# A gated attention and expert kernel on Trainium2: key and query weights multiplied on the chip, and the first stage's five queues in another order

## The chip, the cores and the metric

The kernel runs on one core of one Trainium2 chip. The metric is the device time of one execution in microseconds (us), from the launch's first to its last instruction on that core, the median over several executions. Engines are named as in the profile: PE is TensorE (matrix products and transposes), PEld its weight loads, DVE is VectorE, ACT is ScalarE, POOL is GpSimd, SP is SyncE, which here only starts DMA transfers. Each engine works through its own queue in order; engines wait for each other by semaphores.

## The reference, cut to what matters

Four blocks follow each other on `x` (8 batches of 256 tokens of 256 numbers), each added to `x` with a gain. The change touches the first; what it computes:

```python
# _layernorm(x) is q_in; ctx_512 (8, 120, 128) is key and value input
q = jnp.einsum('bld,de->ble', q_in, Wq) + bq
k = jnp.einsum('bld,de->ble', ctx_512, Wk) + bk
v = jnp.einsum('bld,de->ble', ctx_512, Wv) + bv
scores = jnp.einsum('bqe,bke->bqk', q, k)
attn = jax.nn.softmax(scores, axis=-1)
x = x + jnp.tanh(g_xattn[0]) * jnp.einsum('bqk,bke->bqe', attn, v)
```

The second block is a mixture of experts: logits of 12 experts per token, the best two chosen, eight of the experts real two-layer networks of width 512. The third is attention with 16 heads, the fourth one linear layer in 8-bit floats.

## The kernel before, in words

The first stage of the program does the first attention for the eight batches and, beside it, what the experts need: the logits, and the expert weights (8 MB, loaded in eight 1 MB pieces into `wl`) split into a rounded part `wh` and a rest `wl`. The split has 32 chunks of 512 columns: ACT writes `wh` of chunk j (`high(j)`, L667), and then the rest is written over `wl`: by POOL (`low(j)`, L512, 28 chunks), or by DVE (`low(j)`, L1045, the four chunks of `VECTOR_LOW`). A rest waits for its own high (`split_h`). No expert may start before all 32 are split.

A batch b passes through these steps. DVE takes the mean and variance of its two tiles (`stats0`, L984 to L992), POOL the inverse root (`root0`, L496, L498), ACT applies them (`norm0`, L648). PE transposes the result (`transpose_x0`, L1576), ACT copies it (`copy_xT`, L629). Keys: PE multiplies the context by the key weights (`keys0`, L1550), ACT adds the bias (`copy_kt0`, L622), PE multiplies by the query weights and by the query bias (`keys_by_query`, L1561, L1564), DVE copies both (`copy_kq`, L1004, `copy_bqk`, L1008). PE makes the scores (`scores0`, L1590 with the bias row, L1596), DVE the maximum (`max0_of`, L1019), ACT the exponential (`exp0_of`, L635), PE its transpose (`transpose_prob`, L1605), ACT the copy (`copy_probT`, L642), PE the product with the values (`attend`, L1613; values by `values0`, L1571, and `copy_v0`, L1013). DVE divides and adds to `x` (`add_x1`, L1025, L1028). Then the second norm: `stats1` on DVE (the same lines as `stats0`), `root1` on POOL (the same lines as `root0`), `norm1` on ACT (L657). PE transposes (`transpose_x1`, L1576), DVE copies (`copy_xT1`, L1039), PE multiplies by the gate (`gate_of`, L1630), DVE adds the bias (`logits_of`, L1049). In between ACT once starts five DMAs that clear the expert output (`clear_y`, L680, L683).

The order on each engine is written by hand: every engine has a loop over steps t, and in step t it serves batch t minus an offset of its own. ACT serves `norm1(t - 6)`, POOL `root1(t - 5)`. Highs and lows are strewn between by tables (`HIGH_FROM`, `LOW_FROM`, `LOW_LATE`): ACT does up to four highs a step, from step 2, POOL up to three or four lows.

At the stage's end twelve products for the third block (`products1`, L1638 and L1641 on PE, L722 and L726 on ACT) are fitted in; PE does the first three in the loop and five more ahead of the counting product (L1689, L1692). DVE then picks the two best experts of each token (L1069 to L1133), PE counts (L1689, L1692), DVE turns the counts into slots, beginning with `rows_up` (L1145), and ends with `slot_i` (L1173) and `blk_i` (L1180). POOL gathers by `slot_i` as soon as its lows are done. The experts start behind that.

Of the kernel before, what the change touches and what calls it, by code (L numbers as in the profile page):

```python
# [23 lines left out]
P = 128  # L24
# [66 lines left out]
def build(nc, x, ctxT, wq0T, wk0, wv0, bq0, bk0, bv0, gateT, gbias, wmoe, wq1, wk1, wv1, wo1,  # L91
          bq1, bk1, bv1, bo1, wfT, bf, gains, c_ident, c_tri, c_count, c_token, c_head, out):
    ctx = ExitStack()
    with ctx:
# [87 lines left out]
        kt0 = sb("kt0", [P, 2, C, LK], F32, att)  # L182
# [111 lines left out]
        def sems(names):  # L294
# [11 lines left out]
        (kt_done, kt_ok, kq_done, kq_ok, bqk_ok, v0_done, v0_ok) = sems(  # L306
            "kt_done kt_ok kq_done kq_ok bqk_ok v0_done v0_ok")
# [7 lines left out]
        split_h, split_l, split_d = sems("split_h split_l split_d")  # L315
# [80 lines left out]
        IN_CTX, IN_CON, IN_CST = 16 * 3, 16 * 4, 16 * 6  # L396
# [9 lines left out]


        HIGH_FROM, LOW_FROM = (8, 2, 2, 2), (4, 4, 9, 3)
        EARLY, FAR = TILES - 2 * U, 64 * P
        AHEAD, ZERO_LOADS = 6, 1 + 2 * TILES * D // ZEROS  # L410
        VECTOR_LOW, VECTOR_FROM = (7, 10, 13, 16), 5
        LOW_LATE = {B: 3, B + 1: 4, B + 2: 3, B + 3: 2, B + 4: CHUNKS}
# [61 lines left out]
        def _(pool):  # L474
            pool.dma_start(ident[:], c_ident).then_inc(cst_in, 16)
# [38 lines left out]
            pieces = iter(j for j in range(CHUNKS) if j not in VECTOR_LOW)  # L514

            def low_next(t, k):

                if t >= LOW_FROM[k]:
                    for j in itertools.islice(pieces, 1):
                        low(j)  # L520

            for t in range(B):
                low_next(t, 0)
                low_next(t, 1)
                root0(t)
                low_next(t, 2)
                low_next(t, 3)
                if 0 <= t - 5:
                    root1(t - 5)
            for t in range(B, B + 5):  # L530
                root1(t - 5)
                for j in itertools.islice(pieces, LOW_LATE[t]):
                    low(j)
# [73 lines left out]
        def _(act):  # L607
# [10 lines left out]
            def copy_kt0(b):  # L618
                act.wait_ge(kt_done, b + 1)
                wait(act, kq_done, b - 1)  # L620
                for m in range(C):
                    ins = nc.scalar.activation(kt0[:, b % 2, m, :], bank[5][:, m * LK:(m + 1) * LK], ACT.Identity,  # L622
                                               bias=bk0_sb[:, m:m + 1])
                ins.then_inc(kt_ok, 1)
# [46 lines left out]
            def high_next(t, k):  # L671

                if t >= HIGH_FROM[k]:
                    for j in itertools.islice(pieces, 1):
                        high(j)
# [9 lines left out]
            for t in range(B + 9):  # L685
                if t == B - 1:
                    clear_y()
                if t < B:
                    copy_kt0(t)
                high_next(t, 0)  # L690
                high_next(t, 1)
                if 0 <= t - 3 < B:
                    exp0_of(t - 3)
                if 0 <= t - 6 < B:
                    norm1(t - 6)
                high_next(t, 2)
                if t < B:
                    norm0(t)
                if 0 <= t - 3 < B:
                    copy_probT(t - 3)  # L700
                high_next(t, 3)
                if 0 <= t - 1 < B:
                    copy_xT(t - 1)
# [274 lines left out]
        def _(dve):  # L978
# [22 lines left out]
            def copy_kq(b):  # L1001

                dve.wait_ge(kq_done, b + 1)
                dve.tensor_copy(kq[:, cols(b, C * LK)], bank[1][:, 0:C * LK]).then_inc(kq_ok, 1)  # L1004

            def copy_bqk(b):
                dve.wait_ge(kq_done, b + 1)
                dve.tensor_copy(bqk[0:1, cols(b, LK)], bank[1][0:1, C * LK:(C + 1) * LK]).then_inc(bqk_ok, 1)  # L1008

            def copy_v0(b):  # L1010

                dve.wait_ge(v0_done, b + 1)
                dve.scalar_tensor_tensor(v0[:, b, 0:D], bank[4][0:LK, 0:D], gain[0:LK, 0:1], bv0g[0:LK, :], ALU.mult,  # L1013
                                         ALU.add).then_inc(v0_ok, 1)
# [25 lines left out]

            def low(j):

                dve.wait_ge(split_h, j + 1)
                c = cols(j, CHUNK)
                dve.tensor_tensor(wl[:, c], wl[:, c].bitcast(F32), wh[:, c], ALU.subtract).then_inc(split_d, 1)  # L1045
# [37 lines left out]
            for t in range(B + 9):  # L1083
                if t < B:
                    stats0(t)
                if 0 <= t - 3 < B:
                    copy_bqk(t - 3)
                if t == 3:
# [7 lines left out]
                if 0 <= t - 3 < B:  # L1096
                    copy_v0(t - 3)
                if 0 <= t - 4 < B:
                    max0_of(t - 4)
                if 0 <= t - 8 < B:  # L1100
                    copy_xT1(t - 8)
                if 0 <= t - 5 < B:
                    add_x1(t - 5)
                if t == 9:
                    dve.wait_ge(gate_in, 32)
                if 0 <= t - 9 < B:
                    logits_of(t - 9)
                if t == B + 6:
# [3 lines left out]
                if t == B + 7:  # L1112
# [3 lines left out]
                if 0 <= t - 5 < B:  # L1116
                    stats1(t - 5)
                if 0 <= t - 2 < B:
                    copy_kq(t - 2)
                if 0 <= t - VECTOR_FROM < len(VECTOR_LOW):  # L1120
# [1004 lines left out]
```

## Time and profile before

| | |
|---|---|
| median of 3 executions | 397.42 us (397.18 to 399.65) |
| the profiled execution, its own time | 393.57 us |
| its span, first to last instruction | 391.8 us |
| mean granted clock of TensorE | 0.955 |
| busy, share of the span: PE, DVE, ACT, POOL | 88%, 68%, 59%, 41% |
| first stage, to the last logits | 0 to 75.1 us |
| choice of experts and slots | 75.1 to about 89 us |
| first product of an expert | 93.5 us |

A row of a timeline gives start and duration in us, engine, line, operation, result and operands with their shapes, how many instructions it merges, and in brackets how long the engine sat idle before it and whom it waited for. Durations overlap a little with the next instruction's start, so the pace of an engine is best read from one start to the next. A DMA's or semaphore's name with "issue" means that nothing the profile shows was waited for.

### The profile page before, as it was taken

Reading aid. Unit: us, or ns where it says so; the run is one execution under the profiler, and the core shown is the slowest. Engines: PE = TensorE matmul, PEld = TensorE weight load, DVE = VectorE, ACT = ScalarE, POOL = GpSimd, SP = SyncE. Lnnn points to the kernel's source line nnn. Section 1 sums busy time; section 2 is a strip of 40 time slices with the busy share of each in tenths; the row PEclk is TensorE's granted clock in tenths of the full one; section 3 lists DMA queues with packets and bytes.
Section 4 is the critical chain, followed back from the end, with each engine's and each line's share of the span. In section 5 each row is a group of like instructions: output and inputs, shape, how many; then the busy total and the mean of one; then the engine's idle time right before and its main releaser. Section 6 shows DMA issues by size and latency. Waiting matters only on the chain.

```text
span 391.8 us, 9083 instructions
## 1 busy us (share of the span) xinstructions
PE 345.0 (88%) x2955; PEld 266.9 (68%) x2956; DVE 266.0 (68%) x677; ACT 230.4 (59%) x462; POOL 159.0 (41%) x215
## 2 busy tenths in 40 slices
PE   1989999856899999999999999889999999979185
PEld 1768787644788888888888873656666666656152
DVE  1649879892646655554544566877988898674896
ACT  2398799511454555545555442577578768727685
POOL 6397599503355556555555434312033113000000
PEclk9999999995999999999999999999999999989765
DMA  6998662301223333323223215211011000000014
GB/s 178 337 418 337 259 252 82 109 2 52 60 80 106 132 106 118 98 79 80 74 68 74 66 55 140 90 56 55 12 47 55 2 2 3 3 0 2 0 49 167
DMA packets 15387, 38.26 MB, mean 98 GB/s; under 512 B 3574, under 2 KB 4748, under 8 KB 13820
## 3 DMA queue, kind: packets, MB, share of 16 engines
q1 hardware_dynamic: 9978, 22.55, 16.3%
q0 software_dynamic: 3936, 10.45, 9.2%
q10 hardware_dynamic: 1442, 4.85, 3.2%
q8 instruction: 19, 0.31, 0.3%
q14 instruction: 12, 0.10, 0.1%
HBM read 24.34 MB, written 13.50 MB: 97 GB/s over the span
## 4 chain that ended last, share of the span: by engine, by line
PE 71%; DVE 9%; ACT 8%; DMA 5%; issue 4%; ACTq 1%; SPq 1%; POOL 0%; DVEq 0%
PE two L1739 14%; PE two L1873 5%; PE two L1727 5%; PE two L1728 5%; PE two L1729 5%; PE two L1938 5%; PE two L1758 4%; PE two L1903 4%; PE two L1859 3%; PE two L1839 3%; DMA wl<-in_wmoe 3%; PE two L1749 2%; PE two L1930 2%; PE two L1596 1%; ACT wh L667 1%
## 5 line engine op out<-in xcount | busy, mean ns | idle before, releaser
L539 POOL DMA_INDIRECT xg<-xn_d,slot_i x39 | 37.8, 968 | 65.2 <-PE two L1749 51.1
L1220 DVE SCALAR_TENSOR_TENSOR gate<-th,two 128x512 f32<-128x512 f32 x39 | 26.8, 687 | 42.8 <-ACT th L738 42.8
L1727 PE MATMUL two<-wh,gh 128*128 x156 | 47.2, 303 | 0.2
L545 POOL DMA_INDIRECT y_d<-y_sb,goal_i x39 | 38.5, 987 | 20.5 <-ACT y_sb L748 10.5
L738 ACT ACTIVATE th<-two 128x512 f32<-128x512 f32 x39 | 23.3, 597 | 36.0 <-PE two L1739 36.0
L1728 PE MATMUL two<-wl,gh 128*128 x156 | 44.0, 282 | 0.0
L1729 PE MATMUL two<-wh,gl 128*128 x156 | 43.9, 282 | 0.0
L1758 PE MATMUL two<-ident,gate 128*128 128x128 f32 x156 | 41.9, 272 | 0.5 <-DVE gate L1220 0.5
L559 POOL TENSOR_TENSOR rstd<-var,half 128x2 f32<-128x2 f32 x14 | 9.7, 693 | 79.6 <-DVE var L1287 79.6
L1320 DVE TENSOR_REDUCE nm<-two 128x8 f32<-128x960 f32 x32 | 36.0, 1151 | 4.5 <-PE two L1859 4.1
L512 POOL TENSOR_TENSOR wl<-wl,wh 128x512 fp32r<-128x512 f32 x28 | 35.2, 1276 | 9.0 <-ACT wh L667 9.0
L1739 PE MATMUL two<-wh,xl 128*128 x78 | 37.8, 485 | 0.0
L1739 PE MATMUL two<-wl,xh 128*128 x78 | 37.7, 483 | 0.0
L1739 PE MATMUL two<-wh,xh 128*128 x78 | 34.8, 447 | 2.1 <-DVE xl L1214 2.1
L836 ACT ACTIVATE pT<-two 120x1024 f32<-120x1024 f32 x32 | 31.0, 1039 | 6.3 <-PE two L1873 6.3
L1214 DVE TENSOR_TENSOR xl<-two,xh 128x256 fp32r<-128x256 f32 x39 | 16.6, 425 | 23.4 <-ACT xh L733 23.4
L1727 PEld LDWEIGHTS two<-wh,gh 128*128 128x128 f32 x156 | 29.4, 189 | 3.3 <-issue 0.7
L1728 PEld LDWEIGHTS two<-wl,gh 128*128 128x128 f32 x156 | 29.6, 190 | 0.0
L1729 PEld LDWEIGHTS two<-wh,gl 128*128 128x128 f32 x156 | 29.6, 190 | 0.0
L733 ACT ACTIVATE xh<-two 128x256 fp32r<-128x256 f32 x39 | 15.0, 384 | 23.9 <-PE two L1749 23.8
L1224 DVE TENSOR_TENSOR gl<-two,gh 128x512 fp32r<-128x512 f32 x39 | 26.6, 683 | 0.8 <-ACT gh L743 0.8
L748 ACT ACTIVATE y_sb<-two 128x256 f32<-128x256 f32 x39 | 15.0, 384 | 19.5 <-PE two L1729 19.5
(267 smaller groups left out, 888.4 us busy)
## 6 DMA issues: line engine op xcount, KB each, us to landing
wl<-in_wmoe SPq DMA_DIRECT2D x8, 1024.0 KB, 15.2
y_d<-wh ACTq DMA_DIRECT2D x4, 1024.0 KB
yg<-y_d SPq DMA_DIRECT2D x7, 512.0 KB, 3.6
xn_d<-xq SPq DMA_DIRECT2D x8, 256.0 KB, 2.0
xz<-xn_d SPq DMA_DIRECT2D x8, 256.0 KB, 2.6
out_x<-of SPq DMA_DIRECT2D x8, 256.0 KB, 2.0
x_sb<-in_x SPq DMA_DIRECT2D x1, 1024.0 KB, 7.9
x_sb<-in_x SPq DMA_DIRECT2D x1, 768.0 KB, 4.6
```

What stands on the lines that cost most here:

```text
L512: pool.tensor_tensor(wl[:, c], wl[:, c].bitcast(F32), wh[:, c], ALU.subtract).then_inc(split_l, 1)
L539: pool.indirect_dma_start(xg[:, n % 2, :], None, xn_d, bass.IndirectOffsetOnAxis(ap=slot_i[:, n:n + 1], axis=0)).then_inc(gathered[n % 2], 16)
L545: pool.indirect_dma_start(y_d, bass.IndirectOffsetOnAxis(ap=goal_i[:, n:n + 1], axis=0), y_sb[:, n % 2, :], None).then_inc(y_stored[n % 2] ...
L836: nc.scalar.activation(pT[:, r, p, :], ring(ring_of_keys(b, r) + p)[0:LK, :], ACT.Exp).then_inc(e_ok, 1)
L1220: dve.scalar_tensor_tensor(gate[:, k, :], th[:], 1.0, bank[2 + k][:], ALU.add, ALU.mult).then_inc(gate_ok, 1)
L1224: dve.tensor_tensor(gl[:, k, :], bank[4 + k][:], gh[:, k, :], ALU.subtract).then_inc(gl_ok, 1)
L1320: dve.tensor_reduce(nm[:, u, 2 * HG * p:2 * HG * (p + 1)].rearrange("p (j h) -> p j h", j=2), src.rearrange("p j (h k) -> p j h k", k=LK), ...
L1727: pe.matmul(dst, gh[:, k, a], wh[:, bass.ds(w, D)], start=c == 0, stop=False)
L1728: pe.matmul(dst, gh[:, k, a], wl[:, bass.ds(w, D)], start=False, stop=False)
L1729: ins = pe.matmul(dst, gl[:, k, a], wh[:, bass.ds(w, D)], start=False, stop=c == FC - 1)
L1739: ins = pe.matmul(bank[2 + k][:], (xl if part == 2 else xh)[:, k, c * P:(c + 1) * P], (wl if part == 1 else wh)[:, bass.ds(e + c * FF, FF) ...
L1758: ins = pe.transpose(bank[4 + k][:, c * P:(c + 1) * P], gate[:, k, c * P:(c + 1) * P], ident[:])
```

## The change

The product of key weights and query weights is taken once on the chip (`fold_keys`: transpose `wk0`, multiply by `wq0` and `bq0`, and three small bias terms, `kq_bias`), and the keys of all batches come from four products of 480 columns ahead of the loop, with two more for the bias row (`keys0`). Two of the four results are copied by DVE and two by ACT (`copy_kq0`, `copy_kq1`). `keys0`, `copy_kt0`, `keys_by_query`, `copy_kq` and `copy_bqk` of each batch go. The loops of the five queues get other offsets and another order inside a step, DVE splits no chunk any more, and POOL does all 32 rests. The core of it:

```diff
+            for t in range(-6, B + 3):
+                if 0 <= t - 3 < B:
+                    low_next()
+                if t + 6 < B:
+                    root0(t + 6)
+                if 0 <= t + 2 < B:
+                    low_next()
+                    low_next()
+                if 0 <= t - 1 < B:
+                    root1(t - 1)
+            for j in pieces:
+                low(j)
...
-            for t in range(B + 9):
+            for t in range(B + 7):
                 if t == B - 1:
                     clear_y()
-                if t < B:
-                    copy_kt0(t)
-                high_next(t, 0)
-                high_next(t, 1)
                 if 0 <= t - 3 < B:
-                    exp0_of(t - 3)
+                    high_next()
+                    copy_probT(t - 3)
+                    high_next()
                 if 0 <= t - 6 < B:
                     norm1(t - 6)
-                high_next(t, 2)
+                if 0 <= t - 1 < B:
+                    copy_xT(t - 1)
+                if t == 1:
+                    copy_kq1()
+                if 0 <= t - 2 < B:
+                    exp0_of(t - 2)
+                if 0 <= t - 7 < B:
+                    high_next()
                 if t < B:
                     norm0(t)
...
             for j in pieces:
                 high(j)
...
+            def copy_fold():
+                dve.wait_ge(fold_done, 1)
+                dve.tensor_copy(wkT[:].rearrange("p c n -> p (c n)"), bank[5][:, 0:C * P]).then_inc(fold_ok, 1)
+                dve.wait_ge(fold_done, 2)
+                dve.tensor_copy(qk[:], bank[0][:, 0:D + 1]).then_inc(fold_ok, 1)
...
+            for t in range(-4, B + 7):
+                if t == 0:
+                    copy_kq0()
...
+                if 0 <= t < B:
+                    copy_v0(t)
...
+                if 0 <= t - 5 < B:
+                    copy_xT1(t - 5)
+                if 0 <= t - 2 < B:
+                    stats1(t - 2)
+                if 0 <= t < B:
+                    max0_of(t)
+                if t + 4 < B:
+                    stats0(t + 4)
+                if t == -4:
+                    copy_fold()
+                if 0 <= t - 1 < B:
+                    add_x1(t - 1)
...
+            def keys0():
+                pe.wait_ge(fold_ok, 3)
+                for m in range(C):
+                    for h in range(2):
+                        pe.matmul(bank[2 + 2 * m + h][:, 0:HB], qk[:, m * P:(m + 1) * P], ctxT_sb[:, h * HB:(h + 1) * HB],
+                                  start=True, stop=True).then_inc(fold_done, 1)
...
             def scores0(b):
                 pe.wait_ge(xT_copied, b + 1)
-                pe.wait_ge(kq_ok, b + 1)
-                pe.wait_ge(bqk_ok, b + 1)
+                pe.wait_ge(kq_ok, 4)
+                pe.wait_ge(kq1_ok, 2)
...
+            fold_keys()
+            keys0()
+            for t in range(B + 7):
+                if t == B + 2:
+                    pe.wait_ge(con_in, IN_CON)
+                if 0 <= t - (B + 2) < 3:
+                    products1(t - (B + 2), t - (B + 1))
+                if 0 <= t - 6 < B:
+                    transpose_x1(t - 6)
+                if 0 <= t - 2 < B:
+                    transpose_prob(t - 2)
+                if 0 <= t - 1 < B:
+                    scores0(t - 1)
...
+                if t < B:
+                    transpose_x0(t)
+                if 0 <= t - 2 < B:
+                    attend(t - 2)
...
-            pe.wait_ge(split_l, CHUNKS - len(VECTOR_LOW))
-            pe.wait_ge(split_d, len(VECTOR_LOW))
+            pe.wait_ge(split_l, CHUNKS)
```

How the rows move, on ACT first, behind the `norm1` of batch 3 and to that of batch 7. `wh` is a high, `xq1` is `norm1` (two rows a batch), `prob` the exponential, `probT` a copy. Before:

```order
L667 ACTIVATE wh<-wl 128x512
L642 ACTIVATE probT<-two0 120x256
L667 ACTIVATE wh<-wl 128x512 x3
L635 ACTIVATE prob<-two3,negmax 128x120 x2
L657 ACTIVATE xq1<-x_sb,less1,rstd1 128x256 x2
L667 ACTIVATE wh<-wl 128x512
L642 ACTIVATE probT<-two0 120x256
L667 ACTIVATE wh<-wl 128x512 x3
L657 ACTIVATE xq1<-x_sb,less1,rstd1 128x256 x6
```

After, the same stretch:

```order
L635 ACTIVATE prob<-two3,negmax 128x120 x2
L667 ACTIVATE wh<-wl 128x512 x2
L642 ACTIVATE probT<-two0 120x256
L667 ACTIVATE wh<-wl 128x512
L657 ACTIVATE xq1<-x_sb,less1,rstd1 128x256 x2
L667 ACTIVATE wh<-wl 128x512
L657 ACTIVATE xq1<-x_sb,less1,rstd1 128x256 x2
L667 ACTIVATE wh<-wl 128x512
L657 ACTIVATE xq1<-x_sb,less1,rstd1 128x256 x2
L667 ACTIVATE wh<-wl 128x512
L657 ACTIVATE xq1<-x_sb,less1,rstd1 128x256 x2
L667 ACTIVATE wh<-wl 128x512 x10
```

Before, the last `norm1` stands behind all 32 highs; now 22 stand ahead of it and ten behind.

On POOL, from the `root1` (`rstd1` and `less1`) of batch 4 to the end of the lows (`wl`). Before:

```order
L496 TENSOR_TENSOR rstd1<-var1,half 128x2
L498 TENSOR_TENSOR less1<-less1,rstd1 128x2
L512 TENSOR_TENSOR wl<-wl,wh 128x512 x4
L496 TENSOR_TENSOR rstd1<-var1,half 128x2
L498 TENSOR_TENSOR less1<-less1,rstd1 128x2
L512 TENSOR_TENSOR wl<-wl,wh 128x512 x3
L496 TENSOR_TENSOR rstd1<-var1,half 128x2
L498 TENSOR_TENSOR less1<-less1,rstd1 128x2
L512 TENSOR_TENSOR wl<-wl,wh 128x512 x2
L496 TENSOR_TENSOR rstd1<-var1,half 128x2
L498 TENSOR_TENSOR less1<-less1,rstd1 128x2
L512 TENSOR_TENSOR wl<-wl,wh 128x512 x3
```

After:

```order
L498 TENSOR_TENSOR rstd1<-var1,half 128x2
L500 TENSOR_TENSOR less1<-less1,rstd1 128x2
L514 TENSOR_TENSOR wl<-wl,wh 128x512
L498 TENSOR_TENSOR rstd1<-var1,half 128x2
L500 TENSOR_TENSOR less1<-less1,rstd1 128x2
L514 TENSOR_TENSOR wl<-wl,wh 128x512
L498 TENSOR_TENSOR rstd1<-var1,half 128x2
L500 TENSOR_TENSOR less1<-less1,rstd1 128x2
L514 TENSOR_TENSOR wl<-wl,wh 128x512
L498 TENSOR_TENSOR rstd1<-var1,half 128x2
L500 TENSOR_TENSOR less1<-less1,rstd1 128x2
L514 TENSOR_TENSOR wl<-wl,wh 128x512 x10
```

Before, three lows stood behind the last `root1`; now ten do, and 22 stand ahead of it.

On PE, one step of the loop in the first half of the stage (`bqk` and `kq` are the scores, `v` the product with the values, `xq` the transpose of a normed batch, `prob` that of the exponential, `wv_sb` the values). Before:

```order
L1561 MATMUL two<-kt,wq_sb 128x120 x4
L1564 MATMUL two<-kt,bq_sb 1x120 x2
L1605 MATMUL two<-ident,prob 120x128 x2
L1571 MATMUL two<-wv_sb,ctxT_sb 120x256
L1550 MATMUL two<-ctxT_sb,wk_sb 128x120 x2
L1590 MATMUL two<-bqk,ones 128x240
L1596 MATMUL two<-kq,xT 128x120 x4
L1613 MATMUL two<-v,probT 128x257 x2
L1576 MATMUL two<-ident,xq 128x128 x4
```

After:

```order
L1619 MATMUL two<-ident,prob 120x128 x2
L1604 MATMUL two<-bqk,ones 128x240
L1610 MATMUL two<-kq,xT 128x120 x4
L1590 MATMUL two<-ident,xq 128x128 x4
L1627 MATMUL two<-v,probT 128x257 x2
L1585 MATMUL two<-wv_sb,ctxT_sb 120x256
```

Nine rows have become six: the products with `wk_sb`, `wq_sb` and `bq_sb` are gone from the step.

## Rows read from the trace of the kernel before

**Rows 1.** The chain that ended last, at the end of the first stage.

```profile
74.95 0.20 DVE logit L1049
...
79.84 0.17 DVE rows_up L1145
```

**Rows 2.** Timeline of PE, one step in the middle of the stage.

```profile
31.67 0.67 PE L1590 MATMUL two<-bqk,ones 1*128 1x240 f32 x2
...
33.25 1.04 PE L1613 MATMUL two<-v,probT 120*128 120x257 f32 x4
34.13 0.60 PE L1576 MATMUL two<-ident,xq 128*128 128x128 f32 x4
34.57 1.05 PE L1561 MATMUL two<-kt,wq_sb 128*128 128x120 f32 x8
...
36.05 0.43 PE L1605 MATMUL two<-ident,prob 128*120 128x128 f32 x2
36.32 0.59 PE L1571 MATMUL two<-wv_sb,ctxT_sb 128*120 128x256 f32 x2
36.75 0.60 PE L1550 MATMUL two<-ctxT_sb,wk_sb 128*128 128x120 f32 x4
37.28 0.67 PE L1590 MATMUL two<-bqk,ones 1*128 1x240 f32 x2
```

**Rows 3.** Timeline of ACT, a step and the issue of the clearing DMAs.

```profile
36.80 0.62 ACT L667 ACTIVATE wh<-wl 128x512 fp32r<-128x512 f32 x1
37.32 0.59 ACT L629 ACTIVATE xT<-two 128x512 f32<-128x512 f32 x1
37.80 0.61 ACT L622 ACTIVATE kt<-two,bk_sb 128x120 f32<-128x120 f32 x2
...
39.76 0.61 ACT L635 ACTIVATE prob<-two,negmax 128x120 f32<-128x120 f32 x2 [0.83 <-DVE negmax L1019]
40.27 1.08 ACT L657 ACTIVATE xq<-x_sb,less,rstd 128x256 f32<-128x256 f32 x2
41.25 0.62 ACT L667 ACTIVATE wh<-wl 128x512 fp32r<-128x512 f32 x1
...
45.97 0.61 ACT L622 ACTIVATE kt<-two,bk_sb 128x120 f32<-128x120 f32 x2 [1.85 <-issue]
```

**Rows 4.** Timeline of POOL at the stage's end: lows, the last root, lows.

```profile
66.54 2.51 POOL L512 TENSOR_TENSOR wl<-wl,wh 128x512 fp32r<-128x512 f32 x2
69.00 0.70 POOL L496 TENSOR_TENSOR rstd<-var,half 128x2 f32<-128x2 f32 x1
...
69.93 3.86 POOL L512 TENSOR_TENSOR wl<-wl,wh 128x512 fp32r<-128x512 f32 x3
```

**Rows 5.** Timeline of ACT, the norm of batch 7.

```profile
70.01 1.09 ACT L657 ACTIVATE xq<-x_sb,less,rstd 128x256 f32<-128x256 f32 x2 [2.29 <-POOL less L498]
```

**Rows 6.** Timeline of DVE, one batch's sum and second norm.

```profile
34.33 0.17 DVE L1025 RECIPROCAL rsum<-two 128x2 f32<-128x2 f32 x1 [0.21 <-PE two L1613]
...
35.44 0.75 DVE L984 BATCH_NORM_STATS2 stat<-x_sb 128x6 f32<-128x256 f32 x2
...
36.65 0.40 DVE L1004 COPY kq<-two 128x240 f32<-128x240 f32 x1
```

**Rows 7.** Timeline of DVE, the first steps of the choice of experts.

```profile
70.96 0.40 DVE L1072 TENSOR_TENSOR eq<-logit,top 128x144 f32<-128x144 f32 x1
71.39 1.26 DVE L1073 SCALAR_TENSOR_TENSOR cand<-eq,count 128x144 f32<-128x144 f32 x1
...
74.23 0.31 DVE L1081 SCALAR_TENSOR_TENSOR left<-hot,logit 128x144 f32<-128x144 f32 x1
```

**Rows 8.** The chain that ended last, its first load.

```profile
2.13 5.33 DMA bq_sb<-in_bq
```

**Rows 9.** Timeline of PE, products early in the stage.

```profile
11.61 1.90 PE L1561 MATMUL two<-kt,wq_sb 128*128 128x120 f32 x8
```

More of the change, by code:

```diff
@@ L512, in low, with low_next @@
                 pool.tensor_tensor(wl[:, c], wl[:, c].bitcast(F32), wh[:, c], ALU.subtract).then_inc(split_l, 1)
[L514 to L532, printed above, removed]
-                    low(j)
+            pieces = iter(range(CHUNKS))
+            def low_next():
+                for j in itertools.islice(pieces, 1):
+                    low(j)
+            for t in range(-6, B + 3):
[10 more added lines that the diff above has]
+                low(j)
             pool.wait_ge(slots_kept, 1)
@@ L616, in _, with copy_kq1 @@
             act.wait_ge(ctx_in, IN_CTX)
[L618 to L624, printed above, removed]
+            def copy_kq1():
+                act.wait_ge(fold_ok, 3)
+                for h in range(2):
+                    act.wait_ge(fold_done, 6 + h)
+                    nc.scalar.activation(keys_of_half(1, h), bank[4 + h][:, 0:HB].rearrange("p (b k) -> p b k", k=LK),
+                                         ACT.Identity, bias=kq_bias[:, 1:2]).then_inc(kq1_ok, 1)
             def copy_xT(b):
@@ L669, in _, with high_next @@
             pieces = iter(range(CHUNKS))
[L671 to L675, printed above, removed]
+            def high_next():
+                for j in itertools.islice(pieces, 1):
+                    high(j)
             def clear_y():
@@ L1545, in _, with fold_keys @@
             pe.wait_ge(ctx_in, IN_CTX)
-            def keys0(b):
-                wait(pe, kt_ok, b)
-                for m in range(C):
-                    ins = pe.matmul(bank[5][:, m * LK:(m + 1) * LK], wk0_sb[:, m * P:(m + 1) * P], ctxT_sb[:, cols(b, LK)],
-                                    start=True, stop=True)
-                ins.then_inc(kt_done, 1)
-            def keys_by_query(b):
-                pe.wait_ge(kt_ok, b + 1)
-                wait(pe, kq_ok, b)
-                wait(pe, bqk_ok, b)
+            def fold_keys():
+                pe.wait_ge(ident_in, 16)
+                for c in range(C):
+                    ins = pe.transpose(bank[5][:, c * P:(c + 1) * P], wk0_sb[:, c * P:(c + 1) * P], ident[:])
+                ins.then_inc(fold_done, 1)
+                pe.wait_ge(wq_in, 32)
+                pe.wait_ge(fold_ok, 1)
+                for c in range(C):
+                    pe.matmul(bank[0][:, 0:D], wkT[:, c, :], wq0_sb[:, c, :], start=(c == 0), stop=(c == C - 1))
+                for c in range(C):
+                    ins = pe.matmul(bank[0][:, D:D + 1], wkT[:, c, :], bq0_sb[:, c:c + 1], start=(c == 0), stop=(c == C - 1))
+                ins.then_inc(fold_done, 1)
```

139 lines of the change are left out of this document (48 added, 91 removed).

## The prediction

> **What bounds the kernel now.** I read the page first: PE is busy for 88% of the span, but that is a mean over stages, so I went to the chain that ended last, in order of time. It runs through the first stage to the last logits, which DVE stores at 74.95 us, then through DVE alone to the step `rows_up` at 79.84 [rows 1], and from there by slots to the experts. Everything behind `rows_up` is the same in both kernels and has no slack that a later start could use up. So the question is only when `rows_up` starts.
>
> Inside the stage I read one step on PE. From one bias row product to the next there are 37.28 - 31.67 = 5.61 us without a gap [rows 2]: PE bounds the middle of the stage. At its end it is another engine: the `norm1` of batch 7 on ACT waited 2.29 us for POOL's `less` and started at 70.01 [rows 5]. POOL had two lows in front of that root and three behind it [rows 4]. The reader should keep this wait in mind; it is the one that the change multiplies.
>
> **What is removed.** Per batch, on PE: 36.05 - 34.57 = 1.48 us of `keys_by_query` and 37.28 - 36.75 = 0.53 of `keys0` [rows 2], so 2.01 us, eight times 16.1. A middle step keeps 3.60. On ACT the copy of the keys goes (about 0.5 a batch), on DVE two copies and four lows, which POOL takes over at 1.25 each, 5.0. I credit nothing for all this after the first steps, because another chain takes over; a gain shows only in the rival below.
>
> **What is added ahead.** The fold needs `bq0`, which lands at 2.13 + 5.33 = 7.46 [rows 8]. PE is at half pace there: the eight passes of 1.90 us take 1.05 later [rows 9, 2]. Two products of 257 columns cost 2 x 0.43 x 2 = 1.7, eight of one column at most 0.4 each (3.2, an estimate from the 120-column ones), three round trips to DVE 0.3 each: 13.2. Six products of 480 columns, at 0.43 per 256 [rows 2], cost 0.81 each, 4.9: 18.1. Then transpose and copy of batch 0 (0.60 and 0.48), two ACT copies of 480 columns (1.2, an estimate from the copy of 512): the first scores start at 20.4. Scores 1.58 (33.25 - 31.67), transpose 0.6, copy 0.48, exponential 0.51, `norm0` 0.98 [rows 2, 3]: ACT begins step 3, the first with highs, at 24.5. This could be 2 us off either way.
>
> **Steps 3 to 5.** Two loops compete: exponential, transpose, scores, transpose, copy on PE and ACT (0.3 + 1.6 + 0.6 + 0.5 + 0.6 = 3.6, with handoffs 3.7), and DVE, which in a step with both norms does two statistics of 1.21, the sum of 1.11 [rows 6], maximum and values of 0.4 each: 4.3. One step at 3.7 and two at 4.3 give 24.5 + 12.3 = 36.8 for the start of step 6 on ACT.
>
> **Steps 6 to 13, where the sum is decided.** Count highs on ACT and lows on POOL. Before the `norm1` of batches 0 to 7 ACT has done 8, 10, 13, 16, 19, 20, 21, 22 highs; before the `root1` of the same batches POOL has done 8, 10, 13, 16, 19, 20, 21, 22 lows. They are equal each time. The last low in front of a root waits for the last high in front of the norm, and the norm waits for the root. There is no lead: both engines meet in every step and wait for each other. (In the kernel before the first `norm1` had 13 highs in front of it and its `root1` only seven lows, and the last norms came behind all 32 highs.) What is queued behind the waiting `norm1` on ACT is the copy of the transposed batch, the exponential, the next high and `norm0`, so PE, DVE and again POOL wait too.
>
> Prices: a high 0.52 from start to start, 0.62 to its end, and POOL perhaps 0.1 later; copy 0.48; exponential 0.51; a norm 41.25 - 40.27 = 0.98 [rows 3]; a low (69.00 - 66.54)/2 = 1.23 to 1.25; a root 69.93 - 69.00 = 0.93 [rows 4].
> - Step 6: high to POOL 0.72, two lows 2.5, root 0.93 and handoff: 4.2. Then norm1 0.98, copy 0.48, exponential 0.51, norm0 0.98: 7.15.
> - The five clearing DMAs: 1.9, as ACT's idle time behind them before [rows 3].
> - Step 7: the same and a high more: 7.67.
> - Step 8: of three lows one was started early: 4.2 + 0.98 + 0.48 + 0.51 + 0.52 = 6.69.
> - Step 9: three lows in a row: 0.2 + 3.75 + 0.93 = 4.9, + 0.98 + 0.51 + 0.52 = 6.9. Step 10: 4.9 + 0.98 + 0.52 = 6.4.
> - Steps 11, 12: one low: 2.4 + 0.98 + 0.52 = 3.9 each. Step 13: 2.4 + 0.98 = 3.4.
>
> The sum is 47.9. The last `norm1` ends at 36.8 + 47.9 = 84.7, where before it ended at 70.01 + 0.98 = 70.99: 13.7 us later. (SP's stores of the normed batches wait behind the same norms; they are not in front of anything before the gathers.)
>
> **From the last norm to `rows_up`.** Before, 79.84 - 70.99 = 8.85. Now ten highs stand on ACT behind that norm (5.2), then the small copies (about 1.1), and only then the copies that free banks for `products1`; four products on PE, in front of the counting product, wait for them one after the other: 5.2 + 1.1 + four copies of 0.58 (2.3), the last product 0.5 and the counting 0.9 give 10.0. This is a new wait: 1.15 more, and the bounds are 0, if ACT's copies were not waited for, and 3.0, if PE's four products each waited a full copy and their own 0.45.
>
> Second, POOL still has ten lows, 12.5 us, while DVE chooses the experts. In the trace two DVE operations with both inputs in SBUF began while POOL was in a low: `cand`, of 144 columns, took 1.26 where `left` of the same size took 0.31, and `eq` 0.40, some 0.09 over [rows 7]. Eleven such operations now fall among the ten lows, where before it was these two. Lower end: no loss. Upper end: each loses 0.95, 10.5 in all. I take the mean of the two seen, 0.52, so 5.7; DVE alone would be there 1.9 before PE's counting, so 3.8 of it is on the path (8.6 at the upper end, 0 at the lower).
>
> The Trainium skill, in the GPSIMD Engine Reference under "Key points", says that GpSimd shares its SBUF interfaces with VectorE and that they contend where a DVE instruction has two SBUF inputs; `cand` agrees. By that rule taken strictly all eleven would wait and the sum would stand at its upper end.
>
> **Sum.** 13.7 + 1.15 + 3.8 = 18.65 us. Against the profiled execution, 393.57, this gives 412.2. The median shown lies 3.85 higher, and what will be compared is a median, so I add the same 18.65 to 397.42: 416.1.
>
> **Rivals.**
> - Faster. The mechanism: POOL's work, not the handoff, bounds the stage. If highs ran far enough ahead that POOL never waited from its first low at 25.2, then 22 lows (27.5) and 11 roots (10.2) put the last root at 62.9, the last norm at 63.9 and `rows_up` at 73.9, 5.9 earlier: 391.5. For it: PE loses 16 us of work. Against it: the counts above; it decides from the point where a low's high is ready a low's length earlier. Some 7%.
> - Within 1%. Stage start 3 us earlier and half of the meetings hidden, +2 or so: 399.4. 5%.
> - The meetings hold, but DVE and POOL don't disturb each other: 412.2 (+14.8). For it: `eq` lost only 0.09. 25%.
> - The meetings hold and TensorE falls to its lower clock, as in its early products [rows 9]. PE idles several us in each step from 9 on. Then the tail's transpose and two gates double (+1.3) and so do four products in front of the counting (+1.5 to +2): about 419. 10%.
> - Forecast as summed, 416.1: 53%.
>
> **How the numbers follow.** About 1% is what a measurement of this kernel can tell from no change. Slower by more: 0.53 + 0.25 + 0.10 = 0.88; faster by more 0.07; within 0.05. The range reaches down to 405, which takes in a start 3 us earlier together with no disturbance and some overlap I don't see, and up to 424: the upper end of the disturbance (+4.8) and a start 3 us later.
>
> **What would show it.** In the profile of the changed kernel: ACT's `norm1` (xq from `x_sb`) idles for POOL's `less` eight times, 2 to 3.5 us each, some 20 in total, against 2.29 once; POOL waits for `wh` in most steps; PE is busy for little over half of the second half of the stage; the last `norm1` ends near 84.7 and `rows_up` starts near 98.5; DVE operations with two SBUF inputs take up to 1.3 us while POOL's last ten lows run; `products1` waits for ACT. The parts behind `rows_up` keep their lengths. It would be wrong if `norm1` hardly waits for POOL, or if the last one ends before 75.

## The result, and the profile after

The changed kernel takes 416.73 us in the median (414.33 to 420.04, 4 executions) beside 397.3 (393.67 to 399.65, 4 executions) of the kernel before: slower by 19.4 us or 4.9% between the medians, and with a ratio of 1.0527, 95% interval 1.0458 to 1.0597. Some executions of most kernels here show a lower granted clock and take one to two per cent longer; ratios and intervals leave these out and the medians shown do not, so the two can differ. The forecast was 416.1 and slower. The profiled execution has an own time of 414.33 us, a span of 412.5 and a mean granted clock of TensorE of 0.904; before it was 393.57, 391.8 and 0.955.

The page's busy times and TensorE's granted clock over the 40 slices of the span:

```profile
PE 357.4 (87%) x2861; PEld 270.4 (66%) x2862; DVE 269.3 (65%) x665; ACT 228.0 (55%) x448; POOL 163.6 (40%) x219
PEclk9989967565679999999999999999999999998865
```

PE issues 94 matmuls fewer than before the change and is still busier in microseconds, because its clock reads 5 to 7 tenths in the sixth to the twelfth slice, 52 to 124 us. In the kernel before, the windows read 1.00 up to 75 us. The sum of waits in the first 110 us names what the forecast named:

```profile
ACT xq L657 <- POOL less L500: 21.8, 8, 3.4
POOL wl L514 <- ACT wh L667: 20.7, 11, 4.8
POOL rstd L498 <- DVE var L991: 15.2, 5, 8.8
```

(Columns: who waited for whom, us in total, times, the longest.) The `norm1` waits for POOL eight times, 21.8 us in all; before, in the same stretch, once for 2.29 [rows 5]. And POOL waits for ACT's highs for nearly as long, 20.7 us in all, where before it was 9.0. One such meeting, batch 3, in the timelines of ACT and then of POOL:

```profile
54.62 0.37 ACT L642 ACTIVATE probT<-two 120x256 f32<-120x256 f32 x1
54.88 0.62 ACT L667 ACTIVATE wh<-wl 128x512 fp32r<-128x512 f32 x1
58.25 1.09 ACT L657 ACTIVATE xq<-x_sb,less,rstd 128x256 f32<-128x256 f32 x2 [2.75 <-POOL less L500]
```

```profile
54.79 2.50 POOL L514 TENSOR_TENSOR wl<-wl,wh 128x512 fp32r<-128x512 f32 x2 [0.23 <-ACT wh L667]
57.25 0.69 POOL L498 TENSOR_TENSOR rstd<-var,half 128x2 f32<-128x2 f32 x1
58.02 0.20 POOL L500 TENSOR_TENSOR less<-less,rstd 128x2 f32<-128x2 f32 x1
60.92 3.73 POOL L514 TENSOR_TENSOR wl<-wl,wh 128x512 fp32r<-128x512 f32 x3 [2.71 <-ACT wh L667]
```

ACT ends its high at 55.50. POOL works from 54.79 on two lows and then on the root, and from 55.50 until 58.25, 2.75 us, ACT stands still. At 58.22 POOL is done, and now it stands still for 2.71 us until ACT has normed, copied, taken the exponential and written the next high. The two engines take turns. Where before three lows went on behind a root without a gap [rows 4], here each root is followed by a wait. The end of the chain on ACT and POOL:

```profile
84.19 1.09 ACT L657 ACTIVATE xq<-x_sb,less,rstd 128x256 f32<-128x256 f32 x2 [2.29 <-POOL less L500]
85.19 5.29 ACT L667 ACTIVATE wh<-wl 128x512 fp32r<-128x512 f32 x10
```

```profile
85.88 12.55 POOL L514 TENSOR_TENSOR wl<-wl,wh 128x512 fp32r<-128x512 f32 x10 [1.72 <-ACT wh L667]
```

The last `norm1` ends at 85.17 (84.19 and the 0.98 of a norm), 14.2 us later than before [rows 5]. Ten highs and ten lows stand behind it. DVE, beside these lows:

```profile
87.27 1.27 DVE L1084 TENSOR_TENSOR hot<-cand,pick 128x144 f32<-128x144 f32 x1
...
90.67 0.37 DVE L1078 TENSOR_TENSOR eq<-logit,top 128x48 f32<-128x48 f32 x1
91.07 1.19 DVE L1079 SCALAR_TENSOR_TENSOR cand<-eq,count 128x48 f32<-128x48 f32 x1
...
95.83 1.48 DVE L1078 TENSOR_TENSOR eq<-left,top 128x192 f32<-128x192 f32 x1
97.34 1.30 DVE L1079 SCALAR_TENSOR_TENSOR cand<-eq,count 128x192 f32<-128x192 f32 x1
98.68 0.35 DVE L1083 TENSOR_REDUCE pick<-cand 128x16 f32<-128x192 f32 x1
99.06 0.36 DVE L1084 TENSOR_TENSOR hot<-cand,pick 128x192 f32<-128x192 f32 x1
...
101.16 0.17 DVE L1148 TENSOR_SCALAR rows_up<-two 128x8 f32<-128x8 f32 x1 [0.28 <-PE two L1695]
```

The lows end at 98.43. The `hot` of 192 columns behind that takes 0.36 us; `eq` and `cand` of the same size ahead of it take 1.48 and 1.30. What each loses is about what was left of the low that was running. By the lows' pace of 1.25 us from 85.88 on (an estimate), the `hot` at 87.27 had some 1.1 us of a low in front of it and took 1.27 (0.31 in e2, which has no such lows), and the `eq` at 90.67 had 0.2 and took 0.37 (0.21 in e2). `rows_up` starts at 101.16 instead of 79.84 [rows 1], 21.3 us later. The two profiled times differ by 20.8, so the loss is complete at that point.

### The profile page after: what moved, and what is told of

Read it like the earlier page. It is cut to its first block, busy times and chain, and to the rows that moved or that the text cites. A ratio compares the mean times of both kernels' runs of the same rounds, so it can differ in the third digit from the quotient of the medians.

```text
span 412.5 us, 8859 instructions
## 1 busy us (share of the span) xinstructions
PE 357.4 (87%) x2861; PEld 270.4 (66%) x2862; DVE 269.3 (65%) x665; ACT 228.0 (55%) x448; POOL 163.6 (40%) x219
## 4 chain that ended last, share of the span: by engine, by line
PE 64%; DVE 13%; ACT 8%; POOL 7%; issue 4%; DMA 2%; ACTq 1%; SPq 0%; DVEq 0%
PE two L1741 13%; PE two L1875 5%; PE two L1729 5%; POOL wl L514 5%; PE two L1730 5%; PE two L1731 5%; PE two L1940 4%; PE two L1760 4%; PE two L1905 4%; PE two L1861 3%; PE two L1841 3%; PE two L1751 2%; PE two L1932 1%; POOL rstd L498 1%; PE two L1921 1%
## 5 line engine op out<-in xcount | busy, mean ns | idle before, releaser
L514 POOL TENSOR_TENSOR wl<-wl,wh 128x512 fp32r<-128x512 f32 x32 | 40.1, 1277 | 20.8 <-ACT wh L667 20.7
```

Of the source, the lines that this page charges most:

```text
L514: pool.tensor_tensor(wl[:, c], wl[:, c].bitcast(F32), wh[:, c], ALU.subtract).then_inc(split_l, 1)
```

## The experiments

Eight kernels ran. The positions below are each kernel's own profiled execution; the third column is the start of `rows_up` less the end of the last `norm1` (its start and 0.98). The medians and ratios are those of the timed executions; the kernel before, timed again beside them, read 397.43 or 397.56 beside e1 to e6 and 399.29 beside e7 and e8.

| kernel | last `norm1` starts | `rows_up` starts | between | median us | ratio to before |
|---|---|---|---|---|---|
| before | 70.01 | 79.84 | 8.9 | 397.3 | |
| the changed kernel | 84.19 | 101.16 | 16.0 | 416.73 | 1.0527 (1.0458 to 1.0597) |
| e1, root first | 70.38 | 87.37 | 16.0 | 402.09 | 1.0128 (1.0006 to 1.0249) |
| e2, no last lows | 86.12 | 99.01 | 11.9 | 411.28 | 1.0397 (1.0336 to 1.0457) |
| e5, two highs ahead | 69.55 | 84.96 | 14.4 | 400.95 (397.88, 397.9, 404.0, 404.98) | none given |
| e3, fold in the old order | 69.96 | 79.80 | 8.9 | 392.17 | 0.9894 (0.9854 to 0.9935) |
| e4, e3 with eight rests on DVE | 66.04 | 76.92 | 9.9 | 391.21 | 0.9873 (0.9786 to 0.9961) |
| e6, shared rests | 72.95 | 84.05 | 10.1 | 401.84 | 1.0107 (1.0049 to 1.0165) |
| e7, before with eight rests on DVE | 72.93 | 83.82 | 9.9 | 400.0 | 1.0054 (0.9992 to 1.0115) |
| e8, e4 again | 68.67 | 79.56 | 9.9 | 395.5 | 0.9873 (0.9771 to 0.9975) |

**e1: the root at the head of POOL's step.** Only the place of `root1` in the step moves; the count of lows and highs in front of each norm on ACT stays.

```diff
             for t in range(-6, B + 3):
+                if 0 <= t - 1 < B:
+                    root1(t - 1)
                 if 0 <= t - 3 < B:
                     low_next()
...
-                if 0 <= t - 1 < B:
-                    root1(t - 1)
```

> The changed kernel with one edit: in POOL's loop root1 stands at the head of its step, ahead of the lows of that step, so that 1 to 3 lows fewer stand in front of it and each has a lead over the highs. Theory A (ACT and POOL meet in every step): ACT's wait for less in front of norm1 falls from 21.8 us to under 6, the last norm1 ends near 68 instead of 85.2, and rows_up, still with ten or eleven lows beside it, starts near 84 instead of 101.2: the span falls by about 17 us, to about 396. Theory B (POOL's load of 32 lows and 16 roots is what costs, wherever they stand): the last norm1 ends above 80 and the span falls by under 4 us. Theory C (the lower clock of TensorE stretches the stage): PE becomes busier, the clock rises, but the order on POOL alone gives under 4 us.

Measured: the ratio fell from 1.0527 to 1.0128, and the profiled time from 414.33 to 401.72. The sums of waits of the first 110 us:

```profile
POOL wl L514 <- ACT wh L667: 5.0, 5, 2.3
ACT xq L657 <- POOL less L500: 4.0, 3, 2.9
```

The wait of 21.8 us is 4.0, that of 20.7 is 5.0, and the last `norm1` starts 13.8 us earlier, at 70.38, where the kernel before has it. So the meeting is the cause of the whole delay of the norms. The norm ends at 71.4 and not near 68, as was expected, because the loop began later: in this execution TensorE's clock read 0.50 and 0.62 at 25 to 35 us (0.91 and 1.00 in the changed kernel's), and the last `norm0` ahead of step 6 (it ends ACT's step 5) starts at 40.60 instead of 37.30. Counted from there, the last `norm1` comes after 29.8 us, where the changed kernel takes 46.9. What remains of the loss is what lies behind the last norm, 16.0 us as in the changed kernel instead of 8.9: 7.1 us. The profiled times differ by 8.15.

**e5: two highs ahead.** The reverse test: the root stays where it is, and ACT gets a lead of two chunks, once, at step 2.

```diff
+                if t == 2:
+                    high_next()
+                    high_next()
                 if 0 <= t - 3 < B:
                     high_next()
```

> The changed kernel with one edit on ACT alone: two more highs in step 2, so that ACT is two highs ahead of POOL's lows from there on; POOL's order is untouched and so is the number of lows in front of each root1. Theory A (what costs is that highs and lows have no lead): the first norm1 still waits (its POOL work is late for another reason, root0 of batch 7), the seven behind it wait under 1 us each, ACT's total wait for less falls from 21.8 us to 4 to 8, the last norm1 ends near 71 to 74 instead of 85.2, and the span falls by 10 to 13 us. Theory B (the number of lows in front of a root is what costs, not their lead): as the changed kernel, span within 3 us of it.

Measured: the last `norm1` starts at 69.55 and the profiled time is 397.88. In the timeline of ACT the wait in front of the first norm is 2.73, as ever, then none for two batches, then 0.40 and 0.97, and at the last three:

```profile
65.24 1.09 ACT L657 ACTIVATE xq<-x_sb,less,rstd 128x256 f32<-128x256 f32 x2 [0.53 <-POOL less L500]
67.39 1.09 ACT L657 ACTIVATE xq<-x_sb,less,rstd 128x256 f32<-128x256 f32 x2 [0.54 <-POOL less L500]
69.55 1.09 ACT L657 ACTIVATE xq<-x_sb,less,rstd 128x256 f32<-128x256 f32 x2 [0.54 <-POOL less L500]
```

From norm to norm these take 2.15 us, POOL's low and root (1.23 and 0.93), where the changed kernel takes 3.9. Two instructions that were in the program anyway, issued once earlier, bring 14.6 us at the last norm; counted from the last `norm0` ahead of step 6 it is 31.8 us instead of 46.9. More was gained than expected: 5.7 us of waits are left, as expected, but the norm ends at 70.5 and not at 71 to 74, and the span is 16.5 shorter and not 10 to 13. Neither the number of lows nor the root's place alone makes the meetings, but that there was no lead.

**e2: the last ten lows left out.** This kernel leaves part of the computation away: the rests of the last ten chunks are not written.

```diff
-            pieces = iter(range(CHUNKS))
+            pieces = iter(range(CHUNKS - 10))
...
-            pe.wait_ge(split_l, CHUNKS)
+            pe.wait_ge(split_l, CHUNKS - 10)
```

> The changed kernel without the ten lows that POOL does behind its last root1 (the rests of the last ten chunks are not computed, so that part of the work is left out). Theory A (DVE and POOL shut each other out of SBUF): the DVE operations with two SBUF inputs between the last norm and rows_up go back from 0.9 to 1.5 us to 0.2 to 0.36; rows_up is then bound by ACT's ten highs and the copies for products1, and starts about 10 us behind the last norm1 instead of 16.0: 6 us less. Theory B (the choice of experts is slow for another reason, such as the waiting for PE's counting): under 1.5 us less. Everything ahead of the last norm1 stays as it is, 85.2.

Measured: `rows_up` starts 11.9 us behind the last norm instead of 16.0, so 4.1 us are POOL's disturbance, not 6. (The whole stage is 1.9 us later than in the changed kernel, from the last `norm0` ahead of step 6 on, 39.18 against 37.30; TensorE's clock read 0.50 at 25 to 30 us in this execution.) Two of DVE's `cand` and `rows_up` in this kernel:

```profile
91.80 0.21 DVE L1079 SCALAR_TENSOR_TENSOR cand<-eq,count 128x48 f32<-128x48 f32 x1
...
93.48 0.36 DVE L1079 SCALAR_TENSOR_TENSOR cand<-eq,count 128x192 f32<-128x192 f32 x1
...
99.01 0.17 DVE L1148 TENSOR_SCALAR rows_up<-two 128x8 f32<-128x8 f32 x1 [2.93 <-PE two L1695]
```

0.21 and 0.36 instead of 1.19 and 1.30: the disturbance is gone in full. But DVE then waits 2.93 us for PE's counting: the second limit behind the last norm, `products1` and what it waits for, is 11.9 us long, not the 10.0 of the forecast. Its longest piece behind the ten highs, in the timeline of PE of this kernel, and the same eight products in e3:

```profile
94.06 3.77 PE L1652 MATMUL two<-wv_sb,ctxT_sb 128*120 128x256 f32 x8 [1.32 <-ACT kt L721]
```

```profile
75.52 1.89 PE L1665 MATMUL two<-wv_sb,ctxT_sb 128*120 128x256 f32 x8
```

They take 3.77 us against 1.89, twice as long; the granted clock of the stretch is 0.67 here (90 to 110 us) and 0.89 in e3 (75 to 90 us). The changed kernel, too, takes 3.77.

**e3: the fold in the old order.** The other half of the change alone: `fold_keys`, the wide keys and their copies as in the changed kernel; queues, offsets and tables of highs and lows as before, with four rests on DVE.

```diff
+        HIGH_FROM, LOW_FROM = (8, 2, 2, 2), (4, 4, 9, 3)
+        VECTOR_LOW, VECTOR_FROM = (7, 10, 13, 16), 5
+        LOW_LATE = {B: 3, B + 1: 4, B + 2: 3, B + 3: 2, B + 4: CHUNKS}
```

> The fold and the wide key products alone: the five queues are in the order of the kernel before, with four lows on DVE, and the per-batch key work is gone. Theory A (the fold is cheap, the new order is what costs): faster than before or equal; PE's middle step falls from 5.61 us to what POOL, ACT or DVE allow (about 4.9), the start is 1 to 2 us later, POOL's load of 25 lows and the roots puts the last norm1 near 66 and the span at 387 to 392. Theory B (the fold and the wide products ahead cost more than they save, since they run at half pace before the data is there): the span is at 395 or above.

Measured: 392.17 us, ratio 0.9894 with an interval wholly below 1. The fold alone gains about 1%, as expected. In the profiled execution, though, the last norm ended at 70.9 and not near 66, and the stage ended where it did before (`rows_up` at 79.80 and 79.84), which looked at first as if POOL's work pinned the end. The windows of that execution tell another story (columns: window, its length, busy time and count of PE, PEld, DVE, ACT and POOL, TensorE's granted clock, DMA share, GB/s):

```profile
30.00:35.00 5.00, 3.45 (x21) 2.41 (x19) 4.83 (x16) 2.83 (x7) 4.84 (x7) 1.00 1.02 423
35.00:40.00 5.00, 4.04 (x13) 2.78 (x14) 4.55 (x18) 3.90 (x9) 4.21 (x6) 0.55 0.52 205
40.00:45.00 5.00, 5.00 (x26) 3.88 (x26) 2.92 (x11) 3.94 (x10) 1.60 (x3) 0.77 0.26 103
45.00:50.00 5.00, 3.80 (x24) 2.76 (x23) 4.26 (x14) 3.52 (x9) 4.62 (x6) 1.00 1.00 413
```

In the middle of the stage, after PE had been busy for 3.45 of 5 us, TensorE was granted 0.55 over a window, near its lower level of 1.2 GHz, and POOL stood idle right behind that, at 40 to 45, for want of highs. Ahead of it stands a meeting of DVE and POOL: a rest on DVE began at 31.58, 0.05 us after a low on POOL, and took 1.77 us instead of 0.68; the maximum, the exponential and with it PE came later, and PE stood idle for 2.51 us.

**e4, e7 and e8: eight rests on DVE, with the fold and without.** e4 is e3 with DVE's rests doubled and POOL's late steps shortened; e7 is the kernel before with the same two lines; e8 is e4 again, beside e7.

```diff
-        VECTOR_LOW, VECTOR_FROM = (7, 10, 13, 16), 5
-        LOW_LATE = {B: 3, B + 1: 4, B + 2: 3, B + 3: 2, B + 4: CHUNKS}
+        VECTOR_LOW, VECTOR_FROM = (7, 10, 13, 16, 19, 22, 25, 28), 5
+        LOW_LATE = {B: 2, B + 1: 3, B + 2: 2, B + 3: 1, B + 4: CHUNKS}
```

> e3 (the fold with the queues in the old order) with eight of the 32 lows on DVE instead of four, so that 21 instead of 25 lows stand in front of POOL's last root1. Theory A (in e3 POOL's load pins the last norm1 at 70 us, and that hides what the fold saves on PE): the last norm1 ends near 66 to 67 instead of 71.0, rows_up starts near 76 instead of 79.8, the span falls by 3 to 4 us to about 387. Theory B (another engine is as late as POOL there): the last norm1 stays above 69.5 and the span moves by under 1 us.

> The kernel before with eight rests on DVE instead of four and nothing else; no fold. It asks whether the 2.9 us that the version with the fold and eight DVE rests gained at rows_up needs the fold at all. Theory (POOL's load of rests and roots alone pins the end of the stage, PE's step of 5.61 us is only just as long): the last norm1 ends near 67 to 68 instead of 70.99, rows_up starts at 77 to 78, and the time falls by 2 to 3 us, to a ratio near 0.993. Rival (PE's step and DVE's queue bind as soon as POOL is relieved, since without the fold DVE has two more copies in each step and PE 2.0 us more of products): the last norm1 ends at 70 or later, rows_up at 79 to 81, ratio 0.998 to 1.005, and POOL waits for DVE's var before most of its roots.

> The same kernel as the one with the fold, the old order and eight rests on DVE, repeated beside the run above on the same chip. Both theories of the run above expect of it a last norm1 ending near 67, rows_up near 77 and a ratio of 0.985 to 0.993. If the run above comes out as the theory says, the two differ by less than 1 us; by the rival this one is 2.5 to 4 us faster.

Measured: e4 0.9873, e8 0.9873, e7 1.0054. Without the fold eight rests on DVE gain nothing; with it the kernels are 1.3% faster, against 1.1% with four rests (e3). The bias row products of PE in e7, one step to the next:

```profile
28.86 0.81 PE L1590 MATMUL two<-bqk,ones 1*128 1x240 f32 x2
34.63 0.67 PE L1590 MATMUL two<-bqk,ones 1*128 1x240 f32 x2
40.24 0.67 PE L1590 MATMUL two<-bqk,ones 1*128 1x240 f32 x2
45.86 0.67 PE L1590 MATMUL two<-bqk,ones 1*128 1x240 f32 x2
```

Steps of 5.6 us as before [rows 2]: PE pins e7, and POOL, relieved, waits longer for DVE's `var`, 12.3 us in eight waits instead of 7.1 in five. (The first of these rows is 2.8 us later than in the kernel before, by a stretch of lower clock at 20 to 30 us, and the last `norm1` 2.9 later, so nothing is gained between; `rows_up` is 4.0 later, past the 79 to 81 of the rival. The 5.6 us steps are the reading that doesn't depend on it.) So the rival held in the main: PE's step and POOL's load are about equal in the kernel before, and relieving POOL alone gives nothing. The fold alone (e3), which relieves PE above all, did gain its 1%.

e4 and e8 are one kernel, and their profiled executions differ by 2.64 us at `rows_up`: e4's last norm ended at 67.0, as expected, e8's at 69.65 and not near 67. They part at a rest on DVE, first in e4 and then in e8:

```profile
31.38 0.68 DVE L1062 TENSOR_TENSOR wl<-wl,wh 128x512 fp32r<-128x512 f32 x1
```

```profile
31.62 1.76 DVE L1062 TENSOR_TENSOR wl<-wl,wh 128x512 fp32r<-128x512 f32 x1
```

In both a low on POOL began 0.02 to 0.05 us ahead of it, at 31.36 and 31.57. In e4 it was the low that took longer, 1.84 instead of 1.27; in e8, as in e3, it was the rest. PE starts the transpose of the exponential behind it at 34.67 and 35.99: half of the 2.64 is there before a product runs at a lower clock. Then TensorE is granted 0.55 and 0.77 at 35 to 45 us in e8, and 1.00 and 0.68 in e4, and the other half comes along.

Between the two that run alike, e3 and e8, eight rests on DVE bring 1.3 us at the last `norm1` and 0.24 at `rows_up`. So the 2.9 us by which e4's `rows_up` is ahead of the kernel before are not the eight rests' doing, and 2.6 of them are no more than what two executions of one kernel differ by. Nor did they last: behind `rows_up` e4's execution took 318.0 us (394.92 less 76.92) where the kernel before took 313.7. The 1.1 us that e8's norm gained on e3's and `rows_up` did not is lost on DVE, whose queue has this in front of the last copy of a transposed batch, in e8:

```profile
70.59 0.66 DVE L1089 TENSOR_TENSOR eq<-logit,top 128x144 f32<-128x144 f32 x1
71.29 1.25 DVE L1090 SCALAR_TENSOR_TENSOR cand<-eq,count 128x144 f32<-128x144 f32 x1
72.58 0.69 DVE L1056 COPY xT<-two 128x512 f32<-128x512 f32 x1
```

The copy starts at 72.58; in e3, whose norm came 1.3 us later, at 72.64. `cand` beside POOL's lows holds it. Whether e4 is faster than e3 the times don't tell (0.9873 and 0.9894, with intervals that overlap); both are faster than either kernel of the case, by intervals below 1. No profile shows where the fold's 1% arises: e3's has `rows_up` where the kernel before has it. That stays open.

**e6: all at once.** Root first, three highs in each of ACT's steps, ten rests on DVE strewn over the stage:

```diff
             for t in range(-6, B + 3):
+                if 0 <= t - 1 < B:
+                    root1(t - 1)
                 if t + 6 < B:
                     root0(t + 6)
-                if 0 <= t + 2 < B:
+                if 0 <= t + 2 < B + 3:
                     low_next()
                     low_next()
...
+                if 3 <= t < 13:
+                    low(2 + 3 * (t - 3))
```

> The changed kernel with all three corrections: root1 at the head of POOL's step, three highs a step on ACT from step 3 (all done before the last norm1), and every third low on DVE (10 of 32). If the two mechanisms (no lead; POOL and DVE excluding each other while experts are chosen) are all that was wrong with the new order, the last norm1 ends near 67, rows_up starts near 75 to 77 and the span is near 387 to 389: faster than the kernel before by 1 to 2%. If something else in the new order costs too (its later start, TensorE's lower clock), rows_up starts above 79 and the span is above 391.

Measured: 401.84 us, no better than e1. The expectation was wrong. With no lows behind the stage the tail shrank to 10.1 us as hoped, but two lows stand in front of each of the last roots, and POOL and DVE lose to each other all along. The timeline of POOL in e6:

```profile
59.81 0.68 POOL L498 TENSOR_TENSOR rstd<-var,half 128x2 f32<-128x2 f32 x1
60.58 0.20 POOL L500 TENSOR_TENSOR less<-less,rstd 128x2 f32<-128x2 f32 x1
61.02 3.01 POOL L514 TENSOR_TENSOR wl<-wl,wh 128x512 fp32r<-128x512 f32 x2 [0.24 <-ACT wh L665]
...
67.61 1.14 POOL L498 TENSOR_TENSOR rstd<-var,half 128x2 f32<-128x2 f32 x1
68.83 0.72 POOL L500 TENSOR_TENSOR less<-less,rstd 128x2 f32<-128x2 f32 x1
```

And DVE at the same time:

```profile
67.03 1.17 DVE L1059 TENSOR_TENSOR wl<-wl,wh 128x512 fp32r<-128x512 f32 x1
...
68.81 0.68 DVE L1059 TENSOR_TENSOR wl<-wl,wh 128x512 fp32r<-128x512 f32 x1
```

A root of 0.68 and 0.20 takes 1.14 and 0.72 beside these two rests, and two lows take 3.01 instead of the 2.5 of [rows 4]. A rest on DVE of 0.68 takes 1.17 where it began in a POOL low. The last `norm1` starts at 72.95, 2.6 later than in e1; 0.6 of that is there at the last `norm0` ahead of step 6 (41.21 against 40.60), the rest comes in the loop. Both begin step 6 over 3 us later than the changed kernel; e6's clock read 0.50 and 0.61 at 25 to 35 us.

## Why the prediction was right, point by point

The bound was read rightly: everything hung on when `rows_up` starts, the parts behind it kept their lengths (21.3 us later there, 20.8 in the profiled times).

**The start.** Too early. The fold was ready earlier than forecast: the six products of 480 columns began at 12.28 and not at 13.2. But they had been put at full pace and took 6.8 us instead of 4.9, and the scores behind them 2.1 instead of 1.58. The first scores were forecast at 20.4 and ran at 21.63, ACT began step 3 at 26.83 instead of 24.5, and step 6 at 38.28 instead of 36.8. The step's own range of 2 us either way just misses the 2.3 at step 3; the three steps then ran at 3.74, 3.75 and 3.96 us instead of 3.7 and twice 4.3, which gave 0.85 back: DVE's 4.3 did not set two of them.

**Steps 6 to 13.** Right. Eight meetings were forecast with 2 to 3.5 us each, some 20 in total; there are eight, 2.29 to 3.4 each, 21.8 in total. Their sum, 47.9 from the start of step 6 to the last norm's end, measured 85.17 - 38.28 = 46.9. The 1.5 us that the start was short of and this 1.0 nearly cancel, which is luck: 85.17 against 84.7. The cause is shown from both sides, by the root's place (e1) and by ACT's lead (e5): the first takes away 17.8 of the 21.8 us of waits, the second 16.1.

**From the last norm to `rows_up`.** The mechanism was right and both sizes were low; 13.8 was forecast (8.85, 1.15 and 3.8) and 16.0 measured. The term of `products1`, 1.15, measured 3.05 (11.9 in e2 against 8.85, just over its upper bound of 3.0). The ten highs and the small copies took what they should, to 93.37 in e2. Behind them the sum had 3.7 (four copies, a product and the counting), and 5.6 was measured: not ACT's copies set the pace but PE's own eight products, 3.56 us from the first to the counting, at the lower clock, and the counting took 1.4 instead of 0.9. That was the rival of the lower clock, held at 10%; it came true beside the forecast and not in its place. The disturbance, 3.8 on the path, measured 4.1 beyond that longer term. DVE's own loss had been sized by eleven operations and the mean of the two seen, 0.52 us. Nine fell beside the lows; eight of them lost 0.75 to 1.13 (`cand` of 48 columns 1.19 against 0.21 in e2, `eq` of 192 columns 1.48 against 0.35) and one, the `eq` of 48 columns, 0.16: 0.84 on the mean, near the upper bound of 0.95 and not in the middle. That makes 7.6 us in all against the 5.7 forecast; that the part on the path came out near it is luck, since DVE would have waited longer for PE, 2.93 us (e2) and not 1.9. The mistake was to take the mean of the two seen. The `eq` at 0.40 [rows 7] began at 70.96, with about 0.2 us left of a low (an estimate: lows every 1.28 us from 69.93 on [rows 4]), as the `eq` of 48 columns did here, and most operations begin with more left. The Trainium skill's sentence on the shared SBUF interfaces, in the GPSIMD Engine Reference under "Key points", taken strictly, was the better guide here: all nine lost something here, eight of them 0.75 us or more.

**The sum.** 18.65 forecast, 21.3 at `rows_up`, 20.8 in the profiled times, 19.4 between the medians. The rivals of 391.5 and 399.4 fell with the eight meetings. The credit of nothing for the work removed was right for this kernel, but only because the order used it up: the fold alone gains 1.1% (e3), and the order costs the rest. It was not true, as the forecast's faster rival had it, that a version without meetings would reach `rows_up` at 73.9; e1 and e5, with most of the meetings gone, start it at 87.37 and 84.96. Their last norms end at 71.4 and 70.5 and not at 63.9, and what stands behind takes 16.0 and 14.4 us and not 10.0.

## What to carry to other kernels

Where two in-order queues hand work to each other both ways (highs to POOL, roots back to ACT), count for each waiting instruction how many items the other queue has in front of it on either side: equal counts meant no lead and a wait in every step here, and two items issued once ahead took most of it away. Work taken off one engine can show nothing while a second one of the same length stands beside it, as in e7, where POOL has four rests fewer; look where the time of the relieved one goes. A position in one profile isn't yet an effect: two executions of one kernel lay 2.6 us apart at `rows_up`. And work that is put behind the end of a stage isn't free: here ten lows beside short DVE steps with two SBUF inputs and ten highs in front of copies cost 7 us.

## What was not expected of the hardware

**DVE and POOL hold each other up, one instruction at a time and in both directions.** A DVE operation with two SBUF inputs of 0.17 to 0.36 us took 0.92 to 1.48 beside POOL's lows of 1.25, whatever its size, in eight cases of nine; the loss goes by what is left of the low, not by the operation's own work. And beside a rest on DVE (0.68 us) POOL's `less` took 0.72 instead of 0.20, so moving rests from POOL to DVE (e6) pays part of them twice.

**TensorE's granted clock in a sparse stage.** The windows of the changed kernel, columns as above:

```profile
0.00:20.00 20.00, 12.95 (x40) 7.47 (x41) 8.33 (x33) 2.69 (x5) 9.49 (x27) 1.00 0.81 263
20.00:40.00 20.00, 18.11 (x100) 13.67 (x100) 14.23 (x58) 16.11 (x37) 12.03 (x15) 0.91 0.87 359
40.00:60.00 20.00, 13.99 (x63) 10.42 (x61) 9.30 (x33) 11.10 (x26) 10.28 (x13) 0.83 0.58 236
60.00:75.00 15.00, 12.54 (x61) 9.99 (x60) 6.92 (x26) 7.38 (x17) 9.98 (x11) 0.73 0.14 51
75.00:90.00 15.00, 13.74 (x57) 10.54 (x57) 8.23 (x21) 9.03 (x18) 9.60 (x13) 0.61 0.23 74
90.00:110.00 20.00, 12.31 (x70) 7.98 (x69) 18.64 (x45) 6.79 (x19) 9.48 (x8) 0.59 0.04 13
```

The 0.91 comes from the first half of its window (0.75 at 20 to 25 us, 1.00 from 30 to 50). In the first meetings, at 40 to 45 and 45 to 50 us, PE was busy for 2.40 and 3.68 of 5 us, still at 1.00; at 50 to 60 the clock read 0.66, and it stayed between 0.59 and 0.73 up to 110 us. PE looks 92% busy at 75 to 90 us with 57 matmuls: it is busy because it is slow (the same eight products 3.77 us for 1.89). The clock that is read isn't everything either: the first window reads 1.00, as it does in the kernel before, and yet products run there at half pace [rows 9].

Such a stretch also comes and goes from one execution to the next of one kernel (0.55 and 0.77 at 35 to 45 us in e8, 1.00 and 0.68 in e4), and it can pass for the effect of an edit: two positions of a profile should be compared only where the clock in the windows ahead of them agrees, or counted from a point behind the difference, as was done for e1 and e5.
